# A decoder on one core: the values products of a key tile in one piece of 512 queries, and constant activation biases

## What is computed

```python
def _L1_xattn_ref(x, latents, w_q, w_kv, w_out, b_out):   # 16 heads of 16
    q = latents @ w_q.T
    k, v = jnp.split(x @ w_kv.T, 2, axis=-1)
    attn = jax.nn.softmax(jnp.einsum('blhd,bshd->bhls', q, k) * SCALE, axis=-1)
    out = jnp.einsum('bhls,bshd->blhd', attn, v)
    return out @ w_out.T + b_out
x = _layernorm(x + _L0_attn_ref(...))     # RWKV
x = _layernorm(x + _L0_xattn_ref(x, ctx_1024, mask_BxS2_ik0, ...))
x = _layernorm(x + _L0_ffn_ref(...))
x = _layernorm(x + _L1_attn_ref(...))     # RG-LRU
x = _layernorm(x + _L1_xattn_ref(ctx_1024, x, ...))
x = _layernorm(x + _L1_ffn_ref(...))      # experts
```

## Time and profile before

| | us |
|---|---|
| median of 3 runs | 2336.97 (2332.34 to 2337.36) |
| the profiled execution, its own time | 2334.47 |
| its span, from the first to the last instruction | 2332.6 |
| narrow attention, about | 335 to 590 |
| wide attention, its interleaved units, about | 1127 to 1800 |
| experts, about | 1900 to 2270 |

### The profile page before, as it was taken

One profiled execution on the slowest core, in us unless ns is written; L12 is line 12 of the kernel. 1 busy time (PEld: TensorE's weight loads), 2 busy tenths in 40 slices (PEclk: granted clock), 3 DMA queues, 4 the chain that ended last, 5 costly groups with the idle time before them and its releaser, 6 DMA issues.

```text
span 2332.6 us, 31610 instructions
## 1 busy us (share of the span) xinstructions
PE 1915.1 (82%) x9728; PEld 819.8 (35%) x9729; DVE 1112.3 (48%) x1498; ACT 967.2 (41%) x1638; POOL 221.6 (9%) x188
## 2 busy tenths in 40 slices
PE   5789869999798757727999999999999539999980
PEld 2334323333343222312333333333332326666650
DVE  3652358774212415418877777767760401121115
ACT  2422317667211443310477677667677102222220
POOL 2030100000200103200000000000000240000005
PEclk8889979999899888965999999999999669999995
DMA  7000051011000000092000000000000720000003
GB/s 270 0 0 0 9 124 28 23 27 58 1 0 0 4 0 30 9 133 76 1 15 9 10 13 8 10 14 9 8 2 1 320 72 27 27 27 27 27 25 108
DMA packets 63288, 90.59 MB, mean 39 GB/s; under 512 B 14144, under 2 KB 56320, under 8 KB 61514
## 3 DMA queue, kind: packets, MB, share of 16 engines
q1 hardware_dynamic: 60106, 80.77, 12.0%
q0 software_dynamic: 3072, 8.39, 1.1%
HBM read 61.53 MB, written 27.20 MB: 38 GB/s over the span
## 4 chain that ended last, share of the span: by engine, by line
PE 55%; DVE 6%; issue 4%; POOL 3%; ACT 2%; DMA 2%; SPq 1%; DVEq 0%; ACTq 0%; POOLq 0%
PE ps L1056 9%; PE ps L1014 8%; PE ps L1699 8%; PE ps L512 8%; PE ps L1080 8%; PE ps L1714 5%; DVE arena L1207 2%; PE ps L1357 2%; DMA qparts<-arena 1%; POOL rows_in L1808 1%; PE ps L1115 1%; POOL arena L1813 1%; PE ps L440 1%; PE ps L1707 1%; ACT arena L1767 1%
## 5 line engine op out<-in xcount | busy, mean ns | idle before, releaser
L1162 ACT ACTIVATE arena<-ps 128x512 f32<-128x512 f32 x1088 | 593.8, 598 | 332.7 <-PE ps L1080 331.9
L1207 DVE TENSOR_REDUCE arena<-ps 128x1 f32<-128x802 f32 (+1 forms) x512 | 496.6, 990 | 129.0 <-PE ps L1014 119.9
L512 PE MATMUL ps<-arena 128*128 x832 | 380.6, 618 | 83.9 <-DVE arena L1498 24.5
L1014 PE MATMUL ps<-arena 97*128 97x401 bf16 (+2 forms) x1280 | 356.3, 362 | 80.0 <-DMA arena<-qparts 62.2
L1080 PE MATMUL ps<-arena 100*128 100x512 bf16 x1088 | 370.9, 383 | 9.2 <-issue 8.5
L1056 PE MATMUL ps<-arena 128*32 128x256 f32 x4352 | 349.1, 393 | 0.7 <-ACT arena L1162 0.3
L512 PEld LDWEIGHTS ps<-arena 128*128 128x128 f32 x832 | 163.1, 198 | 299.5 <-issue 299.5
L1699 PE MATMUL ps<-arena 128*128 x608 | 199.1, 470 | 29.2 <-ACT arena L1767 28.4
L1014 PEld LDWEIGHTS ps<-arena 97*128 97x128 bf16 x1280 | 94.7, 99 | 293.8 <-issue 167.2
L1894 DVE TENSOR_TENSOR arena<-ps,arena 128x352 f32<-128x352 f32 x76 | 39.9, 525 | 273.0 <-ACT arena L1774 273.0
L1204 DVE TENSOR_REDUCE arena<-ps 128x2 f32<-128x1024 f32 x128 | 154.3, 1220 | 25.6 <-PE ps L1014 25.6
(11 more groups left out here) (183 smaller groups left out, 1409.9 us busy)
## 6 DMA issues: line engine op xcount, KB each, us to landing
arena<-in_experts_w SPq DMA_DIRECT2D x8, 2176.0 KB, 17.7
arena<-qparts SPq DMA_DIRECT2D x192, 64.0 KB, 2.3
qparts<-arena SPq DMA_DIRECT2D x24, 256.0 KB, 6.0
rows_in<-arena SPq DMA_DIRECT2D x1, 5120.0 KB, 32.7
arena<-kparts SPq DMA_DIRECT2D x12, 416.0 KB, 23.9
arena<-rows_in SPq DMA_DIRECT2D x38, 128.0 KB
rows_out<-arena SPq DMA_DIRECT2D x38, 128.0 KB, 1.7
arena<-in_w_rwkv SPq DMA_DIRECT2D x1, 2560.0 KB, 12.5
```

What stands on the lines that cost most here:

```text
L512: ins = eng.matmul(out, w[:, k, m * P:(m + 1) * P], x[:, k, tok(c)], start=k == 0, stop=k == ktiles - 1)
L1014: ins = eng.matmul(slot_banks(s_static)[:, x, 0:n_keys], Qst[0:97, ring, heads[x], q * P:(q + 1) * P], Kst[0:97, ring * HG + heads[x], at: ...
L1162: eng.activation(probs[:, keys_of(u, kt) % 2, h, :], ring_bank(r), ACT.Exp, bias=0.0).then_inc(ring_read.sem, 1)
L1207: eng.tensor_reduce(MX[:, par, heads[0] * QT + q, n % 2:n % 2 + 1], got, AX.XY, ALU.max).then_inc(slot_free.sem, 1)
```

## The change

It does three things. `PV_CUTS` and `PVW` go: `values` issues one product of 512 columns for each head, and it stands where the first cut stood, between S2 and item B. ACT's copy of the weighted sums hangs on the step ("scores", 0, 3), after its Exp. The five bias columns, their memsets and the wait for them go, and each activation that used one has the constant itself as its bias. Per-feature biases and scales stay.

```diff
@@ attend, plan
-            PV_CUTS = 2
-            PVW = CH // PV_CUTS
...
                     if has_values:
-                        yield ("pv",) + values + (0,)
+                        yield ("pv",) + values
                     if mine[1] is not None:
                         yield ("item", mine[1])
                     yield ("scores", kt, 3)
-                    if has_values:
-                        yield ("pv",) + values + (1,)
@@ PE
-                def values(w, kt, cut):
-                    at = cut * PVW
+                def values(w, kt):
                     for h in range(HG):
-                        ins = eng.matmul(o_bank[32 * h:32 * h + 32, at:at + PVW], Vaug[:, kt, (w % 4) * HG + h, :],
-                                         probs[:, keys_of(w, kt) % 2, h, at:at + PVW],
-                                         start=kt == 0 and cut == 0, stop=kt == n_kt - 1 and cut == PV_CUTS - 1,
+                        ins = eng.matmul(o_bank[32 * h:32 * h + 32, :], Vaug[:, kt, (w % 4) * HG + h, :],
+                                         probs[:, keys_of(w, kt) % 2, h, :], start=kt == 0, stop=kt == n_kt - 1,
                                          skip_group_check=True)
-                    if cut == PV_CUTS - 1:
-                        ins.then_inc(pv_done.sem, 1)
+                    ins.then_inc(pv_done.sem, 1)
...
-                            if kt == 0 and cut == 0 and u > 0:
+                            if kt == 0 and u > 0:
                                 o_copied.wait(eng, i)
-                            values(u + before, kt, cut)
+                            values(u + before, kt)
@@ ACT, unit
                                 invert(u, i, to_invert)
                                 to_invert = None
+                            if step == ("scores", 0, HG - 1) and u > 0:
+                                copy_o(u, i)
...
-                        elif step == ("pv", n_kt - 1, -1, PV_CUTS - 1):
-                            copy_o(u, i)
@@ biases: the same edit at lines 366 to 374, 487 to 496, 546 to 561, 653 to 663, 1368, 1456, 1471 to 1479, 1557, 1761, 1774, 1799
-        eps_col = f32(area(1), 1)
...
-            for col, value in ((eps_col, LN_EPS), (wkv_eps_col, WKV_EPS), (one_col, 1.0), (zero_col, 0.0),
-                               (unscale_col, 0.5 * float(np.log(RMS_SCALE)))):
-                eng.memset(col, value).then_inc(cols_set, 1)
...
-            eng.wait_ge(cols_set, 5)
...
                         eng.activation(norm_rstd[:, tok(c)], bank(c + 4).squeeze(1), ACT.Ln,
-                                       bias=eps_col).then_inc(logged.sem, 1)
+                                       bias=LN_EPS).then_inc(logged.sem, 1)
...
-                eng.activation(silu[:, half, :], ps[:, 2 * half, 0:HALF], ACT.Silu, bias=zero_col).then_inc(e_silu, 1)
+                eng.activation(silu[:, half, :], ps[:, 2 * half, 0:HALF], ACT.Silu, bias=0.0).then_inc(e_silu, 1)
```

More of the change, by code:

```diff
@@ L50 @@
 RMS_SCALE = 2.0 ** 26
+UNSCALE = 0.5 * float(np.log(RMS_SCALE))
 Q_PART = (0, 0, 1, 0, 2, 1)
@@ L365, in _ @@
         def _(eng):
-            eng.wait_ge(cols_set, 5)
             eng.wait_ge(ld_const, 16 * N_CONST)
-            eng.activation(decay, vec["time_decay"], ACT.Exp, bias=zero_col).then_inc(act_const, 1)
+            eng.activation(decay, vec["time_decay"], ACT.Exp, bias=0.0).then_inc(act_const, 1)
             eng.activation(tmp2[:, 0, :], vec["Lam"], ACT.Abs).then_inc(act_const, 1)
             eng.wait_ge(act_const, 2)
-            eng.activation(tmp2[:, 0, :], tmp2[:, 0, :], ACT.Exp, bias=zero_col, scale=-1.0).then_inc(act_const, 1)
+            eng.activation(tmp2[:, 0, :], tmp2[:, 0, :], ACT.Exp, bias=0.0, scale=-1.0).then_inc(act_const, 1)
             eng.wait_ge(act_const, 3)
-            eng.activation(tmp2[:, 0, :], tmp2[:, 0, :], ACT.Ln, bias=one_col).then_inc(act_const, 1)
+            eng.activation(tmp2[:, 0, :], tmp2[:, 0, :], ACT.Ln, bias=1.0).then_inc(act_const, 1)
         @part("dve")
@@ L486, in _ @@
                         eng.activation(norm_rstd[:, tok(c)], bank(c + 4).squeeze(1), ACT.Ln,
-                                       bias=eps_col).then_inc(logged.sem, 1)
+                                       bias=LN_EPS).then_inc(logged.sem, 1)
                     else:
                         guarded.wait(eng, c)
-                        eng.activation(norm_rstd[:, tok(c)], norm_rstd[:, tok(c)], ACT.Ln, bias=zero_col,
+                        eng.activation(norm_rstd[:, tok(c)], norm_rstd[:, tok(c)], ACT.Ln, bias=0.0,
                                        scale=RMS_SCALE).then_inc(logged.sem, 1)
@@ L545, in _ @@
                 mix.wait(eng, c, 2)
-                eng.activation(B2[:, :, tok(c)], ps[:, 2:4, :], ACT.Exp, bias=zero_col).then_inc(w_exp.sem, 1)
+                eng.activation(B2[:, :, tok(c)], ps[:, 2:4, :], ACT.Exp, bias=0.0).then_inc(w_exp.sem, 1)
                 k_sub.wait(eng, c)
-                eng.activation(B3[:, :, tok(c)], B3[:, :, tok(c)], ACT.Exp, bias=zero_col).then_inc(k_exp.sem, 1)
+                eng.activation(B3[:, :, tok(c)], B3[:, :, tok(c)], ACT.Exp, bias=0.0).then_inc(k_exp.sem, 1)
             eng.preload_act_table_set(SIGMOID)
@@ L551, in _ @@
                 r_out.wait(eng, c)
-                eng.activation(B1[:, :, tok(c)], B1[:, :, tok(c)], ACT.Sigmoid, bias=zero_col).then_inc(r_sig.sem, 1)
+                eng.activation(B1[:, :, tok(c)], B1[:, :, tok(c)], ACT.Sigmoid, bias=0.0).then_inc(r_sig.sem, 1)
             eng.preload_act_table_set(LN_EXP)
@@ L556, in _ @@
                 num_scan.wait(eng, c)
-                eng.activation(B3[:, :, tok(c)], B2[:, :, tok(c)], ACT.Ln, bias=wkv_eps_col).then_inc(den_ln.sem, 1)
+                eng.activation(B3[:, :, tok(c)], B2[:, :, tok(c)], ACT.Ln, bias=WKV_EPS).then_inc(den_ln.sem, 1)
             den_ln.wait_all(eng)
             with eng.Fori(0, NC) as c:
-                eng.activation(B3[:, :, tok(c)], B3[:, :, tok(c)], ACT.Exp, bias=zero_col,
+                eng.activation(B3[:, :, tok(c)], B3[:, :, tok(c)], ACT.Exp, bias=0.0,
                                scale=-1.0).then_inc(den_inv.sem, 1)
@@ L660, in _ @@
                     key.wait(eng, c, j + 1)
-                    eng.activation(keys[:, j, :], ps[:, j % 4, :], ACT.Relu, bias=zero_col).then_inc(relu.sem, 1)
+                    eng.activation(keys[:, j, :], ps[:, j % 4, :], ACT.Relu, bias=0.0).then_inc(relu.sem, 1)
                 rec.wait(eng, c)
-                eng.activation(B4[:, :, tok(c)], ps[:, 4:6, :], ACT.Sigmoid, bias=zero_col).then_inc(c_sig.sem, 1)
+                eng.activation(B4[:, :, tok(c)], ps[:, 4:6, :], ACT.Sigmoid, bias=0.0).then_inc(c_sig.sem, 1)
         @part("pool")
@@ L1082, in unit @@
                         elif what == "pv":
-                            _, kt, before, cut = step
+                            _, kt, before = step
                             if before:
@@ L1121, in _ @@
                 ring_read.wait(eng, ring_before(16))
-                for cut in range(PV_CUTS):
-                    values(7, n_kt - 1, cut)
+                values(7, n_kt - 1)
                 denominators(8, 16, 0)
@@ L1367, in _ @@
                     h_done.wait(eng, c, max(j - 1, 0))
-                    eng.activation(ffn_s[:, j % 2, :], ps[:, 2 * (j % 2), :], ACT.Silu, bias=zero_col,
+                    eng.activation(ffn_s[:, j % 2, :], ps[:, 2 * (j % 2), :], ACT.Silu, bias=0.0,
                                    scale=DEQUANT).then_inc(silued.sem, 1)
@@ L1455, in _ @@
                 lin.wait(eng, c)
-                eng.activation(B2[:, :, tok(c)], B1[:, :, tok(c)], ACT.Gelu, bias=zero_col).then_inc(lin_gelu.sem, 1)
+                eng.activation(B2[:, :, tok(c)], B1[:, :, tok(c)], ACT.Gelu, bias=0.0).then_inc(lin_gelu.sem, 1)
             eng.preload_act_table_set(SIGMOID)
@@ L1470, in _ @@
                 for h in range(2):
-                    eng.activation(B4[:, h, tok(c)], B4[:, h, tok(c)], ACT.Exp, bias=zero_col,
+                    eng.activation(B4[:, h, tok(c)], B4[:, h, tok(c)], ACT.Exp, bias=0.0,
                                    scale=rate[:, h:h + 1]).then_inc(a_exp.sem, 1)
@@ L1474, in _ @@
                 a_exp.wait(eng, c)
-                eng.activation(XC[:, :, tok(c)], B4[:, :, tok(c)], ACT.Square, bias=zero_col).then_inc(a_sq.sem, 1)
+                eng.activation(XC[:, :, tok(c)], B4[:, :, tok(c)], ACT.Square, bias=0.0).then_inc(a_sq.sem, 1)
             eng.preload_act_table_set(SQRT)
@@ L1478, in _ @@
             with eng.Fori(0, NC) as c:
-                eng.activation(XC[:, :, tok(c)], XC[:, :, tok(c)], ACT.Sqrt, bias=one_col,
+                eng.activation(XC[:, :, tok(c)], XC[:, :, tok(c)], ACT.Sqrt, bias=1.0,
                                scale=-1.0).then_inc(a_root.sem, 1)
@@ L1556, in _ @@
                 m_sig.wait(eng, c)
-                eng.activation(B1[:, :, tok(c)], B1[:, :, tok(c)], ACT.Gelu, bias=zero_col).then_inc(m_gelu.sem, 1)
```

(5 more changed lines are left out.)

8 lines of the change are left out of this document (2 added, 6 removed).

## The result

The changed kernel takes 2351.54 us (median of 5 runs, 2349.17 to 2356.07) beside 2336.97 us (5 runs) for the kernel before: the ratio is 1.0075 with an interval of 1.0054 to 1.0097, slower. The profiled execution took 2349.96 us with a span of 2348.1. The forecast was 2345.3 in a range of 2324 to 2359, and slower by over 0.2% had 0.6. So the direction and the range hold, while the change costs about twice what was forecast: 0.75% for 0.36%.

A forecast was written before the change was run, and what follows sets the result against it. PE was taken to bound both attentions; its 65 us saving is given back as waits, +12.4, with biases -4.1: +8.3 on the profiled 2334.47 gives 2342.8, median 2345.3 us, range 2324 to 2359.

The forecast's parts named there:

- PE's saving: Values in both attentions: one piece costs 1.10 us against 1.34 for two cuts, 0.24 for each of 272 key tiles, 65 us.
- Rival A: Attentions: the waits do not take hold and PE's saving counts whole, 2268 us; with half the slot waits, 2325; together chance 0.2.
- Slot, wide: Wide tiles with three items: next A needs B's slot, 1.60 us against 1.13 of work; PE waits 0.47, six times a unit.
- Turn: Turn of the maxima, waiting for a reduce: wide 1.60 us behind B, +0.43 in tile 5; narrow 1.92 behind B, +0.06.
- Ring: S2 needs the Exp of the last tile's S3, 1.08 us; a tile without items takes 2.40 against 2.22 before.
- Copy: Values of tile 1 wait for ACT's copy, 1.57 to 1.68 us after S3: taken as 0.23 wide, 0.2 narrow, once a unit.
- Narrow units: Narrow attention: a unit with items gains 0.46 us, -6.4 in 14 units; the last two units +0.47 each, +0.9.
- Waits: 0.42, 0.07, none: PE's ring waits in us between S3 and S2: without items, with A alone (wide), and narrow.
- Biases: Constant biases save 0.09 us per activation; in norms, RWKV, RG-LRU and feed-forward blocks -4.1 us in all, bounds nothing to 7.
- rival D: Activations: constant biases do nothing, as a constant is fetched as a column all the same; 2349 us, chance 0.1.
- half waits: Low end of the range: the 84 wide slot waits are 0.23 us instead of 0.47, time 2325 us.
- a dearer piece: High end of the range: values in one piece cost 0.05 us more each, 14 in all, 2359 us; chance 0.1.

The follow-up runs named there:

- piece_behind_s3: The changed kernel with the one piece of values moved from before item B and S3 to behind S3: 2295.21 us, ratio to the kernel before 0.9841.
- b_late: The changed kernel with the piece behind S3, two cuts kept in each attention's last two units, item B behind S3 in four wide tiles: 2286.60 us, ratio 0.9793.
- half_reduce: The changed kernel with each item's maximum taken over only the first half of its keys: 2285.73 us (one run).
- values_only: The kernel before with the values in one piece, ACT's copy on the step of Exp 3, bias columns kept: 2351.57 us, ratio 1.0074.
- bias_only: The kernel before with constant biases, no bias columns, and the values still in two cuts: 2332.93 us, ratio 0.9997.

## Why the prediction was right, and where its sizes were not

**Right: PE's saving is given back as waits.** Rival A gave 2268. It fails on the place, not on the price: the piece is 1.10 in both orders. The Trainium skill (TensorEngine Tiling (Array Packing), Key Properties) has a change of tiling mode drain TensorE, and halving the changes did save PE work; but in the time it shows only where the work between dependent steps still covers the latencies, and there for 37 us (piece_behind_s3) to 48 us (b_late) of the 65. No run separates the changes of mode from the products and weight loads that went with them.

**The four waits.** *Slot, wide:* 1.60 from B to A and six times 0.47 a unit, as forecast, shown by the time line and by half_reduce. *Turn:* wide 1.60, narrow 1.92 as forecast. *Ring:* 1.07 for the 1.08 worked out, 2.40 for a tile without items. *Copy:* values start at 395.45, 1.65 after S3 at 393.80, within the 1.57 to 1.68 worked out; PE was there at 395.20 (S1 at 394.67, then 0.22 and 0.31), so the wait is 0.25 where 0.2 was taken. The wide unit was +1.0 to +1.2 for +0.95, and the wide units from copy to copy +16.8 for 17.9 less the first unit's 0.7, so 17.2. This part of the sum held. The wide turn of the changed kernel, item B of tile 5 and the turn behind it:

```profile
1224.87 0.51 PE L1002 MATMUL ps<-arena 97*128 97x400 bf16 x2
...
1226.47 0.28 PE L1009 MATMUL ps<-arena 128*16 128x128 f32 x1 [0.87 <-DVE arena L1191]
```

**Narrow units, the first term that failed.** They were to gain 0.46 each and gained 0.23: -1.3 over the attention up to its last copy instead of -5.5, some 4 us. The step "Waits: 0.42, 0.07, none" treated the ring inside a unit only. The time line of the changed kernel at the seam of two narrow units:

```profile
403.94 0.60 PE L1065 MATMUL ps<-arena 100*128 100x512 bf16 x2
...
404.38 0.59 PE L1002 MATMUL ps<-arena 97*128 97x512 bf16 x2
405.01 0.18 PEld L1065 LDWEIGHTS ps<-arena 100*128 100x128 bf16 x2 [0.53 <-ACT arena L1146]
```

S3 starts at 403.94, S0 at 404.16 in the same row, A at 404.38, and S1 at 405.01, 1.07 after S3. A unit has 17 places in a ring of three and the next one starts again at place 0, so S1 takes the bank of the last S3. Work between them is 0.88, so 0.19 of waiting in every unit: with the 0.05 at the copy it accounts for the missing 0.23. The first unit costs 0.4 more at two places: it has no denominators, so its turn was held before already (1.92 from B in both kernels), and the first score of unit 1 was held by the S3 before it as well (1.06 and 1.07). At both the piece adds its 0.43 and no wait gets shorter. No run takes the wait at the seam away; it is read, not tried.

**Behind the wide attention,** a term that was not in the sum: +2.1 in values_only, +1.3 in the changed kernel. The output products (16 fp32) in windows of the kernel before, and of the changed one:

```profile
1800.00:1804.00 4.00, 3.73 (x5) 1.58 (x6) 0.00 (x0) 0.18 (x1) 0.22 (x1) 0.61 0.00 0
1804.00:1809.00 5.00, 5.00 (x12) 1.95 (x10) 0.75 (x1) 0.00 (x0) 0.00 (x0) 0.97 0.00 0
```

```profile
1814.00:1818.00 4.00, 3.54 (x4) 1.51 (x5) 0.00 (x0) 0.37 (x1) 0.41 (x1) 0.50 0.02 4
1818.00:1823.00 5.00, 5.00 (x10) 2.18 (x9) 0.75 (x1) 0.00 (x0) 0.00 (x0) 0.74 0.00 0
```

They begin at 1800.27 and 1814.46, and the granted clock is 0.61 and 0.97 before, 0.50 and 0.74 now: the products run longer at the lower of the two levels (1.2 and 2.4 GHz), 10.20 us for 8.84. Ahead of them PE had waited for the ring in every tile of the last units, which looks like the reason, but two other runs speak against it. Piece_behind_s3 (first row) has these waits too, and b_late (second row) has none:

```profile
1761.94 8.84 PE L1100 MATMUL ps<-arena 128*128 128x512 f32 x16 [2.69 <-POOL arena L1171]
1754.75 10.05 PE L1106 MATMUL ps<-arena 128*128 128x512 f32 x16 [2.69 <-POOL arena L1177]
```

The pause ahead is 2.69 in all of them. So why the clock rose later stays open, and these 1.3 to 2.1 us cannot be put down to the change with certainty.

**Biases, the second term that failed.** The price of one was right: line 661's activations take 598 ns now instead of 687, which is also what the Trainium skill (ScalarE: Activation LUTs, What ACT_TABLE_LOAD costs) gives for a pointer operand, about 93 ns. Back to back it is the same: the four of the earlier trace rows take 3.90 instead of 4.27. So rival D is out. But the sum stopped at ACT. The 16 products of the last chunk of the RG-LRU block, kernel before and then bias_only:

```profile
849.32 7.13 PE L512 MATMUL ps<-arena 128*128 x16 [2.71 <-ACT arena L1464]
```

```profile
847.89 8.54 PE L504 MATMUL ps<-arena 128*128 x16 [2.71 <-ACT arena L1456]
```

The products start 1.43 earlier and take 1.41 longer, at a granted clock of 0.94 instead of 0.97 over the window from 798 to 857: the gain made so far is gone. It is no accident of one trace: these products take 7.13 in all three kernels with bias columns and 8.53 or 8.54 in all six with constants. What makes the clock lower there no run shows. Behind them the activations of the block give the 1.2 of the sum (the products after them follow in 20.27 instead of 21.47). Of -4.1, -1.4 is left in the profiled span and nothing that the runs can tell.

Together: 4 for the narrow units, 1 to 2 behind the wide ones and 3 of biases, less 1 in the wide units, are 7 to 8; the profiled execution took 2349.96 for 2342.8, 7 more. The range was wide for other reasons (half waits, a dearer piece), so that 2351.54 lies inside it is no sign that these terms were foreseen.

## What to carry to other kernels

A piece of work that is moved or merged is priced twice: by what the engine saves, and by the gap it stood in. List for each pair of dependent steps the latency and the work between them (here 1.60 at the slot, 1.08 at the ring), and put the merged piece into the gap that is tight; the seams between units need their own line in that list. Time gained ahead of matrix products after a pause has to be followed through them, since they may run at a lower clock and take it back.

## What was not expected of the hardware

Starting products earlier can leave their end where it was: 16 fp32 products begun 1.43 us earlier ended within 0.02 of the old time, at a lower granted clock, and took the same 8.5 us in every kernel with constant biases. And the weight load's idle time in the waits counts the stream of the product ahead of it (0.84 behind every piece), so the 219.9 us of waits for the reduce are far more than PE lost by it. In the units an estimate from starts is 6 x 0.47 at the slot and 1.0 at the turn, some 54 us in fourteen units.
